# Attention tiles of a fused two-layer kernel: the transposed probabilities are cast and split in one operation per engine instead of two

## The reference, cut to what matters

```
x = x + attention_0(layernorm(x), ctx)   # 16 heads, 73 + 4 keys with two softmaxes
x = x + experts_0(layernorm(x))
x = x + attention_1(layernorm(x), ctx)   # 8 heads, 77 keys, one softmax
x = x + experts_1(layernorm(x))

s = einsum('bhid,bhjd->bhij', q, k) * scale
p = softmax(s); o = einsum('bhij,bhjd->bhid', p, v); out = o @ Wo + bo
```

## Time and profile before

| | |
|---|---|
| device time, 3 runs | 1068.49, 1061.05, 1066.58 us; median 1066.58 us |
| profiled execution | 1069.34 us, of which the span of the instructions is 1067.5 us |
| attention tiles, layer 0 | from about 126 to 276 us |
| attention tiles, layer 1 | from about 760 to 852 us |
| busy over the span | PE 90%, DVE 67%, ACT 45%, POOL 13% |
| mean granted TensorE clock | 0.945 of full speed |

### The profile page before, as it was taken

The page is one execution under the profiler, slowest core; times in us unless marked ns, Lnnn a source line. Parts: engine busy times, 40 slices in busy tenths (PEclk is TensorE's granted clock), DMA queues, the critical chain, the costliest instruction groups (busy, mean ns, idle before and its releaser), DMA issues. The chain is left out here.

```text
span 1067.5 us, 18419 instructions
## 1 busy us (share of the span) xinstructions
PE 960.9 (90%) x6397; PEld 870.8 (82%) x6397; DVE 720.3 (67%) x1262; ACT 483.1 (45%) x897; POOL 142.2 (13%) x128
## 2 busy tenths in 40 slices
PE   4998889999768999999999999966499779999998
PEld 3776679998548999999999999933388747899998
DVE  2334388998429988778877887667587676555665
ACT  0001223333227676667766766401355354455443
POOL 1000022233002860000000000037022100000000
PEclk9999999999858999999999999966699989999999
DMA  8800000000037865665566556033000020000002
GB/s 232 302 0 1 1 1 1 1 1 1 3 97 284 308 240 216 229 239 196 198 238 237 211 198 244 21 107 104 6 1 1 1 80 21 20 21 20 20 2 79
DMA packets 44276, 111.57 MB, mean 105 GB/s; under 512 B 7460, under 2 KB 29702, under 8 KB 35526
## 3 DMA queue, kind: packets, MB, share of 16 engines
q1 hardware_dynamic: 34902, 96.55, 25.6%
q0 software_dynamic: 3072, 8.39, 2.3%
q10 hardware_dynamic: 6256, 6.03, 1.8%
HBM read 90.51 MB, written 18.35 MB: 102 GB/s over the span
## 5 line engine op out<-in xcount | busy, mean ns | idle before, releaser
L93 PE MATMUL e_ps_h<-e_xh,e_w1h 128*128 128x256 f32 x496 | 144.4, 291 | 0.3 <-issue 0.3
L95 PE MATMUL e_ps_h<-e_xh,e_w1l 128*128 128x256 f32 x496 | 141.7, 286 | 0.0
L94 PE MATMUL e_ps_h<-e_xl,e_w1h 128*128 128x256 f32 x496 | 141.7, 286 | 0.0
L93 PE MATMUL e_ps_o<-e_w2h,e_hh 128*128 128x256 f32 x496 | 140.4, 283 | 0.0
L94 PE MATMUL e_ps_o<-e_w2l,e_hh 128*128 128x256 f32 x496 | 140.4, 283 | 0.0
L95 PE MATMUL e_ps_o<-e_w2h,e_hl 128*128 128x256 f32 x496 | 140.4, 283 | 0.0
L1447 ACT ACTIVATE e_hf<-e_ps_h,e_b1s 128x256 f32<-128x256 f32 x248 | 104.2, 471 | 40.8 <-PE e_ps_h L95 33.8
L659 POOL TENSOR_TENSOR at_pr<-at_pr,at_inv 128x1168 f32<-128x1168 f32 (+2 forms) x48 | 58.6, 1235 | 299.2 <-DVE at_inv L606 299.2
L93 PEld LDWEIGHTS e_ps_h<-e_xh,e_w1h 128*128 128x128 f32 x496 | 96.7, 195 | 0.5 <-issue 0.5
L94 PEld LDWEIGHTS e_ps_h<-e_xl,e_w1h 128*128 128x128 f32 x496 | 96.8, 195 | 0.0
L95 PEld LDWEIGHTS e_ps_h<-e_xh,e_w1l 128*128 128x128 f32 x496 | 96.5, 195 | 0.0
(11 more groups left out here) (252 smaller groups left out, 2399.6 us busy)
## 6 DMA issues: line engine op xcount, KB each, us to landing
e_w1s<-in_m_w SPq DMA_DIRECT2D x31, 1024.0 KB
e_w2s<-in_m_w SPq DMA_DIRECT2D x31, 1024.0 KB
slots_in<-zero SPq DMA_DIRECT2D x23, 256.0 KB, 6.5
e_xin<-slots_in SPq DMA_DIRECT2D x23, 256.0 KB
slots_out<-e_yo ACTq DMA_DIRECT2D x23, 256.0 KB, 4.8
X<-in_x SPq DMA_DIRECT2D x1, 2048.0 KB, 24.0
e_xin<-m_xn SPq DMA_DIRECT2D x8, 256.0 KB
d_w1s<-in_m_w SPq DMA_DIRECT2D x8, 256.0 KB, 2.7
```

What stands on the lines that cost most here:

```text
L93: nc.tensor.matmul(out, lh, rh, start=start, stop=False)
L94: nc.tensor.matmul(out, lh, rl, start=False, stop=False)
L95: return nc.tensor.matmul(out, ll, rh, start=False, stop=stop)
```

## The change

The tuple `parts` is gone. ScalarE casts all chunks of a tile in one operation (10 in layer 0, 5 in layer 1), VectorE splits them in one operation, and each semaphore counts one per tile. TensorE waits for the whole split ahead of the first chunk of the out products, and has no wait at chunk 4.

```
-        parts = (slice(0, 4), slice(4, CH))
@@ TensorE
                             wait(pe, s_res, t - 1)
+                            wait(pe, s_plo, t)
                             for ch in range(CH):
-                                for i, cs in enumerate(parts):
-                                    if ch == cs.start:
-                                        wait(pe, s_plo, 2 * t + i - 1)
                                 last = product(nc, ps_o[:, 0:D], (ph[:, ch, :], pl[:, ch, :]),
                                                (Bh[:, b_o, ch, :], Bl[:, b_o, ch, :]), ch == 0, ch == CH - 1)
...
                             wait(pe, s_pn, t + 1)
-                            wait(pe, s_plo, 2 * t)
+                            wait(pe, s_plo, t)
@@ VectorE
-                        for i, cs in enumerate(parts):
-                            wait(dve, s_phi, 2 * t + i + 1)
-                            nc.vector.tensor_tensor(pl[:, cs], probs_t[:, cs], ph[:, cs], ALU.subtract).then_inc(s_plo, 1)
+                        wait(dve, s_phi, t + 1)
+                        nc.vector.tensor_tensor(pl[:], probs_t, ph[:], ALU.subtract).then_inc(s_plo, 1)
@@ ScalarE
-                        for cs in parts:
-                            nc.scalar.copy(ph[:, cs], probs_t[:, cs]).then_inc(s_phi, 1)
+                        nc.scalar.copy(ph[:], probs_t).then_inc(s_phi, 1)
```

## The result

The changed kernel is slower by a little over half a per cent: a median of 1072.6 us in 13 runs (1071.16 to 1079.71) against 1068.92 in 13 runs of the kernel before (1061.05 to 1071.17), ratio 1.0059 with a 95% interval of 1.0035 to 1.0083. On 1068.92 us the ratio is +6.3 us (3.7 to 8.9). The means of the runs, 1073.95 and 1067.68 us, lie the same 6.3 us apart, but the medians only 3.7: some runs of the changed kernel are much slower than its median, and some of the kernel before much faster. The forecast was +6.9 us, and a time of 1073.5.

The account below looks back on a forecast made before the run. Layer 0 was taken as bound by TensorE, layer 1 by a ring through TensorE's wait for the split. Layer 0's +4.9 us and layer 1's +2.1 gave +6.9 on 1066.6, so 1073.5 us, range 1067 to 1080.

Parts of the forecast that it names:

- The ring and its slack: Per tile: out products, residual add, statistics, x, sums, inverse, split, out products; layer 0 8.49 us a tile instead of 8.29.
- an idle of about 0.2 us ahead of the first out product: Sign expected in the changed profile: TensorE in layer 0's loop idle about 0.2 us, released by the split.
- The size of the merged split: VectorE's single split operation per tile: 1.43 to 1.48 us in layer 0, 0.78 to 0.82 in layer 1.
- The lag: TensorE's delay from the end of the awaited split to the out products: 0.05 and 0.14 us in two layer 1 tiles.
- The 1.53 us: Layer 0, start of the merged split to start of the out products: 1.48 to 1.63 us, with 1.53 taken.
- The ends of the layers: Layer 0's first tile +0.56 us, tile 14 +0.75, tile 15 +1.35; layer 1's last tile 0.135 plus +0.11 for its cast.
- Layer 1's written-out tiles: Three tiles of layer 1 offering 0.78, 0.70 and 0.79 us against 0.69 + 0.135: +0.2 us together.
- What was costed at nothing: Saved start-ups, 0.06 us a tile on VectorE, and TensorE's computed wait number at chunk 4: no gain.
- Layer 0 keeps its pace: Rival: layer 0's loop stays at 8.29 us a tile, 2.2 us fall away, 1071.3 us; chance 0.12.
- Fewer operations pay: Rival: VectorE's own work sets the pace, merging frees 0.06 us in each of 32 tiles, 1064.7 us; chance 0.06.
- The matrix clock falls: Rival: new TensorE gaps bring three more half-rate stretches of out products, +12.0 us, 1078.6 us; chance 0.16.

Follow-up runs that it names:

- e5: Changed kernel with the statistics (bn_stats) moved behind the split; ratio 1.0026 against the kernel before, loops 8.27 and 4.84 us a tile.
- e8: Kernel before with a semaphore for each of the two casts, so VectorE's wait number isn't computed; layer 1's loop 5.04 us a tile, one execution.
- e3: Kernel before with casts and splits merged in layer 0 alone; ratio 1.0057, ten loop tiles 84.68 us in layer 0 and 50.87 in layer 1.
- e4: Kernel before with casts and splits merged in layer 1 alone; ratio 1.0019, ten loop tiles 82.74 us in layer 0 and 52.33 in layer 1.
- e2: Kernel before with each tile's cast merged into one operation, split still in two parts; ratio 1.0029, layer 1's loop 5.03 us a tile.
- e1: Kernel before, casts and splits still in two parts, but TensorE waits for both split parts before the out products; ratio 1.0059.
- e7: Kernel before with layer 1's cast in one operation and its split in parts of 2 and 3 chunks instead of 4 and 1; ratio 0.9976.
- e10: e7 with layer 0's split in parts of 2, 2 and 6 chunks, its casts staying 4 and 6; ratio 0.9956 against the kernel before.
- e9: e7 with the statistics moved behind the split; layer 1's loop 4.93 us a tile, in one execution.

## Why the prediction was right, step by step

**The ring and its slack.** Right. It was read from four starts of the timeline, and e5 showed it by taking a piece off the ring: 8.49 to 8.27 and 5.23 to 4.84 us a tile. In layer 0 the 1.33 us that TensorE came after the start of the split were exceeded by a wait of 1.58. One sign that the prediction named did not come: an idle of about 0.2 us ahead of the first out product. The profile shows at most 0.02 there, and only the starts of the matmuls (0.14 us apart before, 0.38 after) tell the wait.

**The size of the merged split.** 1.43 us, as worked out. For layer 1 I had 0.82 and it was 0.77: the first part's 0.685 held 0.045 us that didn't belong to its elements. e8 gives them to the number that VectorE computes for the wait, which the change removes there. The lag I had at 0.10 with 0.05 and 0.14 as ends; with merged splits it was 0.14 or 0.15 in nearly all tiles. The 1.53 us from the start of the split to the products is 1.43 + 0.10 and not, as the prediction says, the middle of 1.48 and 1.63, which is 1.55 or 1.56; measured were 1.57 and 1.58. In layer 1 the two errors cancel (+0.127 us a tile against 0.135), in layer 0 a tile took 8.53 us where I had 8.49. In three of its ten tiles the add followed the products after 3.80 us instead of 3.94 and the tile took 8.39 to 8.41, so that the mean is again 8.49. That it meets the forecast to the hundredth is luck: a lag that was too short and a piece that was too long in three tiles.

**The ends of the layers.** Right in each term for layer 0: +0.54 (from e3 and e4; nothing in the changed kernel's own trace) for 0.56, +0.81 for 0.75, +1.32 for 1.35, of which 0.65 is the cast (e2) where I had 0.66.

**Layer 1's written-out tiles** were mis-sized: the first two steps between adds grew by 0.34 us (9.79 to 10.13), of which I had half. The sum held the 0.78, 0.70 and 0.79 us that these tiles offer against 0.69 + 0.135 and left the lag out. The products started 0.92 us after the start of the split in all three, 0.77 of operation and 0.15 of lag, so they paid 0.5 us together where I had 0.2.

**The time.** The +6.9 us lies near the ratio's +6.3 and inside its interval. That the time itself, 1073.5 us, is within 1 us of the median of 1072.6 is partly luck: the base of 1066.6 was 2.3 us below the later median of the kernel before, and the medians differ by 3.7 us only.

**What was costed at nothing.** The freed time of VectorE brought nothing, as argued. The number for TensorE's wait at chunk 4 brought nothing that a tile shows. The number on VectorE's side did count, 0.045 us a tile in layer 1; I had dismissed only TensorE's and not looked at VectorE's.

**The rivals.** "Layer 0 keeps its pace" is out: 84.94 us. "Fewer operations pay" is out by e1, e7 and e10: the first has as many operations as the kernel before and is as slow as the changed one, the others have as many and more on VectorE and are faster. "The matrix clock falls" is out for the loops, where the granted clock was 1.00 with gaps in every tile, but not for the end of layer 0, where two of the four traces that wait for the whole split hold eleven or twelve and one fifteen more half-rate matmuls; at 0.21 instead of 0.12 us each that is 1.0 to 1.4 us, and not three stretches. The fourth, the changed kernel's own, holds none more. That the longer wait brings them is suggested by these counts and not shown. I can't say how often it happens in the timed runs, since only one execution of each kernel was traced.

The Trainium skill, Perfetto Trace Analysis ("Optimizing Scalar/DVE Operations"), says that breaking instructions up may let work complete sooner where the engine isn't saturated but makes others wait. The traces agree in layer 1, with 5.23 us a tile for one split, 5.10 for two and 4.77 for two with a shorter first (e7), and at the end of layer 0, with 8.42 and 6.10 us against 8.70 and 6.35 (e10). In layer 0's loop the number of operations doesn't decide, but whether the first part is done when TensorE comes, 1.33 us after the start of the split.

## What to carry to other kernels

Ask of a split operation who waits for its first part, and look for the ring through that wait; the cost of merging is the growth of the first part less the ring's slack, and the start-up that is saved counts only where the engine isn't waiting elsewhere on the ring. The first part should be as short as the consumer's work on it covers the next part. Price the first and last tiles apart: here they made 2.7 of the 4.9 us of layer 0 (0.54 of it by e3 and e4), since little or nothing overlaps there.

## What the runs showed that I had not expected

- A number computed ahead of a wait on VectorE costs time on the ring even where the semaphore has long been raised: in layer 1's loop the operation behind it took 685 ns with it and 640 without, and the tile 5.10 and 5.04 us (before and e8). In layer 0's loop the same number costs nothing that can be seen (628 ns in both); why it differs was not tested.
- Taking work off one ring can lengthen another through the exponentials: e9, 4.93 us a tile, is slower than e7, 4.77.
